# The inverse of Q's magnitude as a power of minus one on GpSimd instead of reciprocals on VectorE

## The chip, the cores and the metric

The kernel runs on one core of a Trainium2 chip. A core has TensorE (matrix products into PSUM banks; its weight loads are shown as PEld), VectorE (DVE), ScalarE (ACT), GpSimd (POOL), and a queue engine SyncE (SP) that starts transfers. The engines run their own instruction streams in order and wait for each other through semaphores. The metric is the device time of one execution in microseconds (us).

## The reference

Input x is 2 x 4096 tokens of 512 numbers, fp32. Two residual layers:

- Attention by binding: `y = layernorm(x)`; `Q, K, V = unit(y W + b)`, where `unit(f)` goes to the frequency domain, divides by `|f| + 1e-8` and comes back; `out = unbind(cumsum(bind(K, V)), Q)`, where bind and unbind are products of spectra (with the conjugate for unbind), and the running sum goes over the 4096 tokens of a sequence; `x = x + out`.
- Feed-forward: `layernorm(x)` times W_in gives 8 trees of 255 nodes each; the signs of the logits pick one path of 8 nodes in each tree; the silu of the logits on the path times W_out is added to x.

The kernel folds the Fourier transform into the projection weights, so the projections give real and imaginary parts directly, and everything up to the running sum and its product with Q stays in the frequency domain.

## The kernel before

8192 tokens are done in 32 blocks of T = 256. A step `step(s, ...)` works on three blocks at once: it projects block n = s + 1 and forms its running sum (`proj`), transforms block s back and adds the residual (`inv`), and does the feed-forward of block i = s - 1 (`ffn`). The first three steps (s = -1, 0, 1) and the last four are written out, those between run in a loop. All 32 steps with `proj` do what follows; 30 of them also have `ffn`. The order of the work on each engine is that of the code; nothing reorders it.

TensorE, in a step: the projections of Q, K and V (L416, banks `bank_p`), the inverse transform of block s (`bank_i`), then the trees: for t = 0 to 7, logits of tree t (L455, 24 products), and one tree later the counts of tree t (L464, products of the path matrix with the decisions `dec`), then the output products (L480). So counts of tree 0 come right behind the logits of tree 1.

The magnitudes, for q in Q, K, V (256 tokens times 2 groups of frequencies, 128x512 in `mag`): ScalarE takes the real and imaginary parts out of PSUM (L569 to L580) and squares them (L589, `square`); GpSimd adds the two squares (L783, `sum_squares`); ScalarE takes the square root (L593, `root`). For Q and K GpSimd adds epsilon (L788, `add_eps`). K's and V's magnitudes are multiplied and inverted on VectorE (L875, L881, `kv_denominator`, `kv_inverse`). Q's is inverted by two reciprocals of 128x256 on VectorE (L869, `q_inverse`), and GpSimd multiplies Q by it (L806, L807). The squares share one buffer, so `square` of the next of Q, K, V waits for `sum_squares` of the one before.

ScalarE's order in a step: parts and square of Q, real part of K, root of Q, rest of K and its square, real part of V, root of K, rest of V and its square, root of V, then the copy `odd` (L730) of half the inverse transform, then the silus of the eight trees.

VectorE's order in a step: low halves of the layer norm (L863), the two reciprocals for Q, `unfold` (L968 to L977, it needs `odd`), the decision of tree 0 (L948, `decide`), the residual (L982 to L986), the decision of tree 1, K's and V's denominator, and so on with decisions, low halves of the activations (L954), running sums (L911, L914).

GpSimd's order in a step: `sum_squares` and `add_eps` of Q, the same for K, the two multiplications of Q (they wait for the reciprocals), `sum_squares` of V, then the products of K and V (L816 to L819), and those of Q with the running sum (L824 to L835). In the first step a reduction over the partitions (L774) for the scale of the last weights stands between `add_eps` of Q and `sum_squares` of K.

Of the kernel before, what the change touches and what calls it, by code (L numbers as in the profile page):

```python
# [5 lines left out]
P = 128  # L6
# [4 lines left out]
T = 256  # L11
# [19 lines left out]
ALU = mybir.AluOpType  # L31
ACT = mybir.ActivationFunctionType
F32 = mybir.dt.float32
F16 = mybir.dt.float16
# [17 lines left out]
Q, K, V, G_IN, G_OUT = range(5)  # L52
# [14 lines left out]
def build(nc, x, wq, wk, wv, b_qkv, w_in_t, b_in_t, w_out_t, dft, table_hi, table_lo, table_sp, path_d,  # L67
          flags, keep_d, out):
    with ExitStack() as ctx:  # L69
        def sb(name, shape, dt=F32):  # L70
            return ctx.enter_context(nc.sbuf_tensor(name, shape, dt))
# [29 lines left out]
        s_act = sb("s_act", [P, 1])  # L101
        s_out = sb("s_out", [P, 1])
        off = sb("off", [P, 1])

        mx = sb("mx", [P, GROUPS, 2, 6])
        mxp = sb("mxp", [P, GROUPS])
# [8 lines left out]
        def take(words):  # L115
            spot[0] += words
            return arena[:, spot[0] - words:spot[0]]
# [3 lines left out]
        mag = take(3 * 2 * T).rearrange("p (x c t) -> p x c t", x=3, c=2)  # L121
# [83 lines left out]
        consts_done = sem("consts_done")  # L205
# [24 lines left out]
        den_ready = sem("den_ready")  # L230
        kv_den_ready = sem("kv_den_ready")
        rinv_ready = sem("rinv_ready")
# [530 lines left out]
        @block.gpsimd  # L763
        def _(pool):
            pool.memset(mx[:, :, :, :], 0.0).then_inc(cleared, 1)
            pool.memset(ln_eps[:, :], LN_EPS * X_SCALE ** -2).then_inc(cleared, 1)
            pool.memset(sp_raw[:, :], 1.0)
            pool.memset(zero[:, :], 0.0)
            pool.memset(carry[:, :], 0.0)
            pool.memset(sp_carry[:, :], 0.0).then_inc(cleared, 1)  # L770

            def over_partitions(g):
                pool.wait_ge(grp_max, g + 1)
                pool.partition_all_reduce(mxa[:, g:g + 1], mxp[:, g:g + 1], P, RMAX).then_inc(grp_all, 1)  # L774

            for g in (Q, K, V, G_IN):
                over_partitions(g)

            pool.wait_ge(wf_lo_done, 3)

            def sum_squares(n, q):
                pool.wait_ge(sq_ready, 3 * n + q + 1)
                pool.tensor_tensor(mag[:, q].rearrange("p c t -> p (c t)"), sq[:, 0:2].rearrange("p c t -> p (c t)"), sq[:, 2:4].rearrange("p c t -> p (c t)"), ALU.add).then_inc(ss_ready, 1)  # L783

            def add_eps(n, q):
                pool.wait_ge(consts_done, 1)
                pool.wait_ge(root_ready, 3 * n + q + 1)
                pool.tensor_scalar(mag[:, q], mag[:, q], eps_s[:, q:q + 1], 1.0 / ROOT_DOWN, ALU.add,  # L788
                                   ALU.mult).then_inc(den_ready, 1)

            def step(s, proj, inv, ffn, near, far):
                n = s + 1
                if proj:
                    sum_squares(n, Q)
                    add_eps(n, Q)
                    if not inv:
                        over_partitions(G_OUT)
                    if inv:

                        pool.wait_ge(kv_den_ready, n)
                    sum_squares(n, K)
                    add_eps(n, K)

                    pool.wait_ge(rinv_ready, 2 * n + 2)
                    pool.tensor_tensor(raw[:, Q, 0:2], raw[:, Q, 0:2], mag[:, Q], ALU.mult)  # L806
                    pool.tensor_tensor(raw[:, Q, 2:4], raw[:, Q, 2:4], mag[:, Q], ALU.mult).then_inc(q_hat_ready, 1)  # L807
                    sum_squares(n, V)

                    pool.wait_ge(k_hat_ready, n + 1)  # L810
                    kr, ki, vr, vi = raw[:, K, 0:2], raw[:, K, 2:4], raw[:, V, 0:2], raw[:, V, 2:4]
                    if inv:

                        pool.wait_ge(z_hi_ready, 2 * n)
                        pool.wait_ge(z_lo_ready, n)
                    pool.tensor_tensor(prod[:, 0], kr, vr, ALU.mult)  # L816
                    pool.tensor_tensor(prod[:, 1], ki, vi, ALU.mult)
                    pool.tensor_tensor(prod[:, 2], kr, vi, ALU.mult)
                    pool.tensor_tensor(prod[:, 3], ki, vr, ALU.mult).then_inc(bound, 1)  # L819

                    pool.wait_ge(cum_ready, n + 1)
                    pool.wait_ge(q_hat_ready, n + 1)
                    qr, qi, sr, si = raw[:, Q, 0:2], raw[:, Q, 2:4], cum[:, 0:2], cum[:, 2:4]
                    pool.tensor_tensor(prod[:, 0], sr, qr, ALU.mult)  # L824
                    pool.tensor_tensor(prod[:, 1], si, qi, ALU.mult)
                    pool.tensor_tensor(prod[:, 2], si, qr, ALU.mult)
                    pool.tensor_tensor(prod[:, 3], sr, qi, ALU.mult).then_inc(z_prod, 1)
                    pool.wait_ge(z_prod, n + 1)
                    pool.tensor_tensor(prod[:, 0], prod[:, 0], prod[:, 1], ALU.add)
                    pool.tensor_tensor(prod[:, 2], prod[:, 2], prod[:, 3], ALU.subtract).then_inc(z_sum, 1)  # L830
                    pool.wait_ge(z_hi_ready, 2 * n + 1)
                    pool.wait_ge(z_sum, n + 1)
                    pool.tensor_tensor(z_lo[:, 0:2], prod[:, 0], z_hi[:, 0:2], ALU.subtract)  # L833
                    pool.wait_ge(z_hi_ready, 2 * n + 2)
                    pool.tensor_tensor(z_lo[:, 2:4], prod[:, 2], z_hi[:, 2:4], ALU.subtract).then_inc(z_lo_ready, 1)  # L835

            steps(pool, step)

        @block.vector
        def _(dve):  # L840
# [18 lines left out]
            def low(b, xn, have, done):  # L859

                for j in range(J):
                    dve.wait_ge(have, J * b + j + 1)
                    dve.tensor_tensor(xn_pair[:, j, 1, :], xn[:, j, :], xn_pair[:, j, 0, :],  # L863
                                      ALU.subtract).then_inc(done, 1)

            def q_inverse(n, h):

                dve.wait_ge(den_ready, 2 * n + Q + 1)
                dve.reciprocal(mag[:, Q, h], mag[:, Q, h]).then_inc(rinv_ready, 1)  # L869

            def kv_denominator(n):

# [264 lines left out]
            def step(s, proj, inv, ffn, near, far):  # L1137
                n, i = s + 1, s - 1
                if near:
                    low(s + 2, xn1, xn1_hi_ready, xn1_lo_ready)  # L1140
                if proj:
                    for h in range(2):
                        q_inverse(n, h)
                if inv:
                    unfold(s)
                if ffn:
                    decide(i, 0)
                if inv:
                    residual(s)
                if ffn:  # L1150
                    decide(i, 1)
                if proj:
                    kv_denominator(n)
                    kv_inverse(n, 0)
                if ffn:
                    decide(i, 2)
                if proj:
                    kv_inverse(n, 1)
                if ffn:
                    act_low(i, 0)  # L1160
                    decide(i, 3)
                if proj:
                    k_scale(n)
                    if not inv:
                        for c in range(PIECES):
                            win_low(c)
                if ffn:
                    act_low(i, 1)
                    decide(i, 4)
                    act_low(i, 2)  # L1170
                if inv:
                    stats(s, x1, st2, mv2, ln2_stat, ln2_mv)
                if ffn:
                    decide(i, 5)
                    act_low(i, 3)
                    decide(i, 6)
                    act_low(i, 4)
                    decide(i, 7)
                    act_low(i, 5)
                if proj:  # L1180
                    running_sum(n)
                if ffn:
                    act_low(i, 6)
                    act_low(i, 7)
                if proj:
                    special_unit(n)
                    special_sum(n)
                    special_product(n)
                if proj and not inv:
                    wout_low(0)  # L1190
                    wout_low(1)
                if inv and not ffn:
                    wout_low(2)
                    wout_low(3)
                if inv:
                    scale_and_shift(s, mv2, rs2, nb2, ln2_std, ln2_rstd, ln2_nb)
                    low(s, xn2, xn2_hi_ready, xn2_lo_ready)
                if ffn:
                    result(i, 0)
                if far:  # L1200
                    dve.wait_ge(x_loaded, 16 * (s + 4))
                    stats(s + 3, xa, st1, mv1, ln1_stat, ln1_mv)
                    scale_and_shift(s + 3, mv1, rs1, nb1, ln1_std, ln1_rstd, ln1_nb)
                if ffn:
                    result(i, 1)
# [82 lines left out]
```

## Time and profile before

| | |
|---|---|
| median of 3 runs | 2157.69 us (2157.49 to 2158.01) |
| profiled execution | 2157.28 us |
| its span in the trace | 2155.3 us |
| TensorE busy | 2030.2 us (94%) |
| VectorE busy | 1446.2 us (67%) |
| ScalarE busy | 1179.5 us (55%) |
| GpSimd busy | 805.5 us (37%) |

The span is the time from the first to the last instruction in the trace; the execution's own time is 2.0 us longer. "Busy" is the time in which an engine works on an instruction, and idle time has a releaser: the instruction whose semaphore ended the wait. The granted clock of TensorE is 1.0 at 2.4 GHz and 0.5 at 1.2 GHz. The profile follows the chain that ended last back from the last instruction; through most of the span it runs over TensorE, whose products stand back to back. The first 220 us, in which weights are folded and split and the first blocks fill the pipeline, have long idle stretches on TensorE; behind them it is full.

### The profile page before, as it was taken

What the parts mean: (1) busy time and instruction counts of PE and PEld (TensorE: products, weight loads), DVE (VectorE), ACT (ScalarE), POOL (GpSimd) and SP (SyncE); (2) the same over time, 40 slices, a digit from 0 to 9 for tenths busy, and PEclk for the clock granted to TensorE, in tenths of its full rate; (3) what the DMA queues carried; (4) which work ended last, traced back from release to release, by engine and by line L of the source; (5) the groups of instructions that cost most, each with busy time, mean ns of one, the idle gap of its engine ahead of it and who ended that gap; (6) DMA issues with size and microseconds to landing.
All of it is one profiled execution on the core that took longest, in us unless ns stands there. A gap on an engine that the chain in (4) does not pass through costs nothing. (4 is left out here: it accounts for less than half of the span.)

```text
span 2155.3 us, 40151 instructions
## 1 busy us (share of the span) xinstructions
PE 2030.2 (94%) x15360; PEld 1477.8 (69%) x15360; DVE 1446.2 (67%) x2223; ACT 1179.5 (55%) x1994; POOL 805.5 (37%) x623
## 2 busy tenths in 40 slices
PE   7513999999999999999999999999999999999999
PEld 4312777777777777777777777777777777777766
DVE  3776666667777666677776666777766667777652
ACT  3443565555555655555556555555565555555642
POOL 0054434343344343433443434334434343344310
PEclk9856999999999999999999999999999999999999
DMA  7301122211211222112112221121122211211110
GB/s 270 102 16 33 37 60 59 58 49 49 58 24 53 58 58 58 49 49 58 24 53 58 58 58 49 49 58 25 53 58 58 58 49 49 58 25 45 40 45 25
DMA packets 174212, 118.30 MB, mean 55 GB/s; under 512 B 138466, under 2 KB 138850, under 8 KB 173666
## 3 DMA queue, kind: packets, MB, share of 16 engines
q1 hardware_dynamic: 174178, 117.83, 19.1%
q8 instruction: 23, 0.38, 0.1%
q14 instruction: 11, 0.09, 0.0%
HBM read 50.69 MB, written 16.78 MB: 31 GB/s over the span
## 5 line engine op out<-in xcount | busy, mean ns | idle before, releaser
L455 PE MATMUL bank_l<-arena,win_mem 128*128 128x256 f16 x6144 | 707.3, 273 | 0.0
L480 PE MATMUL bank_l<-wout_mem,arena 128*128 128x512 f16 x3072 | 673.5, 379 | 0.0
L455 PEld LDWEIGHTS bank_l<-arena,win_mem 128*128 128x128 f16 x6144 | 600.0, 98 | 69.0
L416 PE MATMUL bank_p<-arena,wf_hi 128*128 128x256 f16 x3072 | 514.7, 276 | 105.8 <-ACT arena L569 92.0
L480 PEld LDWEIGHTS bank_l<-wout_mem,arena 128*128 128x128 f16 x3072 | 300.6, 98 | 348.8
L416 PE MATMUL bank_p<-arena,wf_lo 128*128 128x256 f16 x1536 | 423.2, 276 | 0.0
L416 PEld LDWEIGHTS bank_p<-arena,wf_hi 128*128 128x128 f16 x3072 | 303.4, 99 | 151.8 <-ACT arena L569 80.2
L603 ACT ACTIVATE arena<-bank_l,bias_in,s_logit 128x256 f32<-128x256 f32 x512 | 260.9, 560 | 263.2 <-PE bank_l L464 263.2
L557 ACT ACTIVATE arena<-arena,nb,rs 128x512 f32<-128x512 f32 x128 | 97.1, 806 | 361.5 <-DVE nb L856 361.5
L954 DVE SCALAR_TENSOR_TENSOR arena<-arena,s_act 128x512 f16<-128x512 f32 x256 | 253.7, 1001 | 3.5 <-ACT arena L612 3.5
L783 POOL TENSOR_TENSOR arena<-arena 128x512 f32<-128x512 f32 x96 | 121.7, 1268 | 330.1 <-ACT arena L589 315.5
L869 DVE RECIPROCAL arena<-arena 128x256 f32<-128x256 f32 x64 | 107.7, 1724 | 191.3 <-POOL arena L788 191.3
L816 POOL TENSOR_TENSOR arena<-arena 128x512 f32<-128x512 f32 x32 | 56.0, 1750 | 407.5 <-DVE arena L887 407.5
L612 ACT ACTIVATE arena<-arena,s_act 128x512 f16<-128x512 f32 x256 | 184.8, 722 | 10.4
L948 DVE TENSOR_SCALAR dec<-bank_l,thr,off 128x256 bf16<-128x256 f32 x256 | 134.9, 527 | 47.4 <-PE bank_l L455 47.4
L416 PEld LDWEIGHTS bank_p<-arena,wf_lo 128*128 128x128 f16 x1536 | 152.0, 99 | 19.2
L968 DVE TENSOR_TENSOR arena<-bank_i,odd 128x254 f32<-128x254 f32 x32 | 13.5, 422 | 222.1 <-ACT odd L730 222.1
L863 DVE TENSOR_TENSOR xn_pair<-arena,xn_pair 128x512 f16<-128x512 f32 x128 | 82.7, 688 | 110.6 <-ACT xn_pair L564 110.6
L833 POOL TENSOR_TENSOR arena<-arena 128x512 f16<-128x512 f32 x32 | 39.1, 1223 | 207.6 <-ACT arena L750 207.6
L900 DVE TENSOR_TENSOR sp_hat<-sp_raw,sp_den 1x256 f32<-1x256 f32 x96 | 115.0, 1198 | 2.0
L824 POOL TENSOR_TENSOR arena<-arena 128x512 f32<-128x512 f32 x32 | 54.2, 1694 | 163.4 <-DVE arena L914 163.4
L881 DVE RECIPROCAL arena<-arena 128x256 f32<-128x256 f32 x64 | 111.6, 1746 | 1.1
(109 smaller groups left out, 2372.2 us busy)
## 6 DMA issues: line engine op xcount, KB each, us to landing
arena<-in_x SPq DMA_DIRECT2D x64, 512.0 KB, 3.4
arena<-arena SPq DMA_DIRECT2D x32, 512.0 KB, 3.2
out<-arena SPq DMA_DIRECT2D x64, 256.0 KB, 2.1
wout_mem<-in_w_in_t SPq DMA_DIRECT2D x1, 4096.0 KB, 22.0
win_mem<-in_w_out_t SPq DMA_DIRECT2D x1, 4096.0 KB, 21.1
arena<-in_w_out_t SPq DMA_DIRECT2D x1, 4096.0 KB, 17.2
arena<-xn_pair SPq DMA_TRANSPOSE x128, 3.2
arena<-in_dft SPq DMA_DIRECT2D x1, 1024.0 KB, 4.9
```

The lines of the kernel that those rows point to most:

```text
L416: mm = pe.matmul(bank, a, b, start=(n == 0), stop=(n == len(pairs) - 1))
L455: mm = pe.matmul(bank_l[t % 4][:, c * T:(c + 1) * T], a[:, k, w:w + P], x2t[:, :, b, k, :], start=(c == 0 and k == 0 and m == 0), stop=(c ...
L480: mm = pe.matmul(bank_l[j][:, :], a[:, m, tok], w[:, m, :], start=(m == 0 and a is a_hi and w is wout_hi), stop=(m == 2 * TREES - 1 and a ...
L557: act.activation(dst[:, j, :], src[:, j, :], ACT.Identity, bias=nb[:, j:j + 1], scale=rs[:, j:j + 1]).then_inc(done, 1)
L603: ins = act.activation(acts[:, t % HELD, c * T:(c + 1) * T], bank_l[t % 4][:, c * T:(c + 1) * T], ACT.Silu, bias=bias_in[:, c, t:t + 1], s ...
L612: act.activation(a_hi[:, 2 * t:2 * t + 2, :], acts[:, t % HELD, :].rearrange("p (c t) -> p c t", c=2), ACT.Copy, scale=s_act[:, 0:1]).then ...
L783: pool.tensor_tensor(mag[:, q].rearrange("p c t -> p (c t)"), sq[:, 0:2].rearrange("p c t -> p (c t)"), sq[:, 2:4].rearrange("p c t -> p ( ...
L869: dve.reciprocal(mag[:, Q, h], mag[:, Q, h]).then_inc(rinv_ready, 1)
L881: dve.reciprocal(mag[:, V, h], mag[:, V, h]).then_inc(kv_rinv_ready, 1)
L900: ins = dve.tensor_tensor(sp_hat[0:1, q, :], sp_raw[s, :], sp_den[s, :], ALU.mult)
L948: dve.tensor_scalar(dec[:, t % HELD, :], bank_l[t % 4][:, 0:T], thr[:, t:t + 1], off[:, 0:1], ALU.is_gt, ALU.mult).then_inc(dec_ready, 1)
L954: dve.scalar_tensor_tensor(out=a_lo[:, m, :], in0=acts[:, t % HELD, :].rearrange("p (c t) -> p c t", c=2), scalar=s_act[:, 0:1], in1=a_hi[ ...
```

## The change

The two reciprocals of Q's denominator leave VectorE. In their place GpSimd raises the whole 128x512 to the power of minus one, element by element, with an exponent tile `minus_one` (128x512 fp16, filled once at the start), directly behind `add_eps` of Q. GpSimd's multiplications of Q then wait for GpSimd's own power.

```diff
--- before.py
+++ after.py
@@ -101,6 +101,7 @@
         s_act = sb("s_act", [P, 1])
         s_out = sb("s_out", [P, 1])
         off = sb("off", [P, 1])
+        minus_one = sb("minus_one", [P, 2, T], F16)
 
         mx = sb("mx", [P, GROUPS, 2, 6])
         mxp = sb("mxp", [P, GROUPS])
@@ -765,6 +766,7 @@
             pool.memset(mx[:, :, :, :], 0.0).then_inc(cleared, 1)
             pool.memset(ln_eps[:, :], LN_EPS * X_SCALE ** -2).then_inc(cleared, 1)
             pool.memset(sp_raw[:, :], 1.0)
+            pool.memset(minus_one[:, :, :], -1.0)
             pool.memset(zero[:, :], 0.0)
             pool.memset(carry[:, :], 0.0)
             pool.memset(sp_carry[:, :], 0.0).then_inc(cleared, 1)
@@ -788,12 +790,17 @@
                 pool.tensor_scalar(mag[:, q], mag[:, q], eps_s[:, q:q + 1], 1.0 / ROOT_DOWN, ALU.add,
                                    ALU.mult).then_inc(den_ready, 1)
 
+            def q_inverse(n):
+                pool.wait_ge(consts_done, 1)
+                pool.wait_ge(den_ready, 2 * n + Q + 1)
+                pool.tensor_tensor(mag[:, Q], mag[:, Q], minus_one[:, :, :], ALU.pow).then_inc(rinv_ready, 1)
 
             def step(s, proj, inv, ffn, near, far):
                 n = s + 1
                 if proj:
                     sum_squares(n, Q)
                     add_eps(n, Q)
+                    q_inverse(n)
                     if not inv:
                         over_partitions(G_OUT)
                     if inv:
@@ -802,7 +809,7 @@
                     sum_squares(n, K)
                     add_eps(n, K)
 
-                    pool.wait_ge(rinv_ready, 2 * n + 2)
+                    pool.wait_ge(rinv_ready, n + 1)
                     pool.tensor_tensor(raw[:, Q, 0:2], raw[:, Q, 0:2], mag[:, Q], ALU.mult)
                     pool.tensor_tensor(raw[:, Q, 2:4], raw[:, Q, 2:4], mag[:, Q], ALU.mult).then_inc(q_hat_ready, 1)
                     sum_squares(n, V)
@@ -862,11 +869,6 @@
                     dve.wait_ge(have, J * b + j + 1)
                     dve.tensor_tensor(xn_pair[:, j, 1, :], xn[:, j, :], xn_pair[:, j, 0, :],
                                       ALU.subtract).then_inc(done, 1)
-
-            def q_inverse(n, h):
-
-                dve.wait_ge(den_ready, 2 * n + Q + 1)
-                dve.reciprocal(mag[:, Q, h], mag[:, Q, h]).then_inc(rinv_ready, 1)
 
             def kv_denominator(n):
 
@@ -1138,9 +1140,6 @@
                 n, i = s + 1, s - 1
                 if near:
                     low(s + 2, xn1, xn1_hi_ready, xn1_lo_ready)
-                if proj:
-                    for h in range(2):
-                        q_inverse(n, h)
                 if inv:
                     unfold(s)
                 if ffn:
```

On GpSimd, the loop's step from the sum of squares of Q (L783) to the two multiplications of Q (L806, L807), before. TENSOR_SCALAR is `add_eps`:

```order
77 L783 TENSOR_TENSOR arena<-arena 128x512
78 L788 TENSOR_SCALAR arena<-arena,eps_s 128x512
79 L782 REGISTER_ALU
80 L783 TENSOR_TENSOR arena<-arena 128x512
81 L788 TENSOR_SCALAR arena<-arena,eps_s 128x512
82 L805 ISA
83 L806 TENSOR_TENSOR arena<-arena 128x512
84 L807 TENSOR_TENSOR arena<-arena 128x512
```

The same place after the change:

```order
81 L785 TENSOR_TENSOR arena<-arena 128x512
82 L790 TENSOR_SCALAR arena<-arena,eps_s 128x512
83 L795 ISA
84 L796 TENSOR_TENSOR arena<-arena,minus_one 128x512
85 L784 REGISTER_ALU
86 L785 TENSOR_TENSOR arena<-arena 128x512
87 L790 TENSOR_SCALAR arena<-arena,eps_s 128x512
88 L812 REGISTER_ALU
89 L813 TENSOR_TENSOR arena<-arena 128x512
90 L814 TENSOR_TENSOR arena<-arena 128x512
```

The power (L796) has come between epsilon of Q and the sum of squares of K; the order is otherwise the same.

On VectorE, the same step before, from the low half of the layer norm (L863) to the decision of tree 0 (L948):

```order
229 L863 TENSOR_TENSOR xn_pair<-arena,xn_pair 128x512
230 L868 ISA
231 L869 RECIPROCAL arena<-arena 128x256 x2
232 L966 REGISTER_ALU
233 L968 TENSOR_TENSOR arena<-bank_i,odd 128x2x127
234 L969 TENSOR_TENSOR arena<-bank_i,odd 128x2x127
235 L970 TENSOR_TENSOR arena<-odd,bank_i 128x2x127
236 L971 TENSOR_TENSOR arena<-odd,bank_i 128x2x127
237 L974 REGISTER_ALU
238 L976 TENSOR_TENSOR arena<-bank_i,odd 128x2x2
239 L977 TENSOR_TENSOR arena<-bank_i,odd 128x2x2
240 L942 ISA
241 L948 TENSOR_SCALAR dec<-bank_l,thr,off 128x256
```

After the change the two reciprocals (row 231) are gone there, and the unfolding follows the low half.

## Rows read from the trace of the kernel before

**Rows 1.** The page: busy time, 40 slices and granted clock of TensorE.
```profile
PE 2030.2 (94%) x15360; PEld 1477.8 (69%) x15360; DVE 1446.2 (67%) x2223; ACT 1179.5 (55%) x1994; POOL 805.5 (37%) x623
...
PE   7513999999999999999999999999999999999999
...
PEclk9856999999999999999999999999999999999999
```

**Rows 2.** Timeline of GpSimd, middle step: start us, us, what [idle before <- releaser].
```profile
1025.59 0.69 POOL L788 TENSOR_SCALAR arena<-arena,eps_s 128x512 f32<-128x512 f32 x1 [0.83 <-ACT arena L593]
1028.88 1.27 POOL L783 TENSOR_TENSOR arena<-arena 128x512 f32<-128x512 f32 x1 [2.59 <-ACT arena L589]
1030.98 0.69 POOL L788 TENSOR_SCALAR arena<-arena,eps_s 128x512 f32<-128x512 f32 x1 [0.83 <-ACT arena L593]
1031.75 1.27 POOL L806 TENSOR_TENSOR arena<-arena 128x512 f32<-128x512 f32 x1
...
1034.21 1.27 POOL L783 TENSOR_TENSOR arena<-arena 128x512 f32<-128x512 f32 x1
```

**Rows 3.** Timeline of ScalarE, the same step.
```profile
1030.18 0.63 ACT L593 ACTIVATE arena<-arena 128x512 f32<-128x512 f32 x1 [0.47 <-POOL arena L783]
...
1035.51 0.63 ACT L593 ACTIVATE arena<-arena 128x512 f32<-128x512 f32 x1 [1.17 <-POOL arena L783]
1036.04 0.58 ACT L730 ACTIVATE odd<-bank_i 128x512 f32<-128x512 f32 x1
```

**Rows 4.** Timeline of VectorE, then TensorE's weight loads, the same step.
```profile
1026.32 3.36 DVE L869 RECIPROCAL arena<-arena 128x256 f32<-128x256 f32 x2 [5.96 <-POOL arena L788]
1036.72 0.42 DVE L968 TENSOR_TENSOR arena<-bank_i,odd 128x254 f32<-128x254 f32 x1 [7.04 <-ACT odd L730]
...
1038.19 0.53 DVE L948 TENSOR_SCALAR dec<-bank_l,thr,off 128x256 bf16<-128x256 f32 x1
...
1038.78 0.11 PEld L464 LDWEIGHTS bank_l<-dec,path 128*128 128x128 f16 x2 [0.37 <-DVE dec L948]
```

**Rows 5.** Waits, whole span: engine line <- releaser: us in total, times, longest.
```profile
POOL mxa L774 <- DVE mxp L1040: 79.4, 4, 44.8
...
PEld bank_l L464 <- DVE dec L948: 19.1, 60, 0.4
```

**Rows 6.** Timeline of GpSimd, steps of blocks 0, 1 and 2.
```profile
100.31 0.38 POOL L774 PARTITION_ALL_REDUCE mxa<-mxp  x1 [6.36 <-issue]
107.55 1.26 POOL L783 TENSOR_TENSOR arena<-arena 128x512 f32<-128x512 f32 x1 [6.86 <-issue]
...
168.17 1.27 POOL L783 TENSOR_TENSOR arena<-arena 128x512 f32<-128x512 f32 x1 [3.09 <-ACT arena L589]
...
228.49 1.27 POOL L783 TENSOR_TENSOR arena<-arena 128x512 f32<-128x512 f32 x1 [3.27 <-ACT arena L589]
```

**Rows 7.** Groups by line: out<-in shapes xcount | busy us, mean ns | idle before.
```profile
L783 POOL TENSOR_TENSOR arena<-arena 128x512 f32<-128x512 f32 x96 | 121.7, 1268 | 330.1 <-ACT arena L589 315.5
L869 DVE RECIPROCAL arena<-arena 128x256 f32<-128x256 f32 x64 | 107.7, 1724 | 191.3 <-POOL arena L788 191.3
...
L863 DVE TENSOR_TENSOR xn_pair<-arena,xn_pair 128x512 f16<-128x512 f32 x128 | 82.7, 688 | 110.6 <-ACT xn_pair L564 110.6
```

**Rows 8.** TensorE after three idle stretches; then windows: us, PE busy, PEclk, DMA.
```profile
46.20 14.14 PE L410 MATMUL bank_l<-arena 128*128 128x512 f32 x29 [6.30 <-ACT arena L618]
...
67.48 0.38 PE L416 MATMUL bank_p<-arena,wf_hi 128*128 128x256 f16 x2 [2.42 <-issue]
...
85.28 0.59 PE L416 MATMUL bank_p<-arena,wf_hi 128*128 128x256 f16 x2 [12.41 <-ACT arena L569]
...
46.20:50.20 4.00, 4.00 (x6) 0.64 0.00 0
67.48:71.48 4.00, 4.00 (x37) 1.00 0.00 0
85.28:91.28 6.00, 6.00 (x34) 0.60 0.95 249
```

## The prediction

> **What bounds the kernel now.** I read the page first. TensorE is busy 94% of the span, and from the fifth of the forty slices on it shows nines in time and in granted clock [rows 1]: time is lost only where something makes TensorE wait. The kernel repeats one step (a block of 256 tokens is projected while an older one is in the feed-forward part); 32 steps project a block, and in 30 of them the decision trees run too. So I looked for the chain inside a step that ends nearest to TensorE, with the timelines of one middle step.
>
> The chain runs over Q, K and V in turn. GpSimd adds the squares (L783), ScalarE takes the root (L593), GpSimd adds epsilon (L788). For Q that ends at 1025.59 + 0.69 = 1026.28. GpSimd then has nothing until ScalarE has squared K: it idles 2.59 us and starts L783 of K at 1028.88. From there it has no gap worth the name: root of K at 1030.18, epsilon at 1030.98, two multiplications from 1031.75, sum of squares of V at 1034.21 to 1035.48 [rows 2]. The root of V waits for exactly that (1.17 us of idle on ScalarE, released by L783), and behind it in ScalarE's order stands the copy `odd` at 1036.04 [rows 3]. VectorE's unfolding (L968) waits for `odd` at 1036.72, the first tree decision (L948) stands behind the unfolding at 1038.19, and TensorE's first count (L464) waits for the decision, 0.37 us of idle at 1038.78 [rows 4]. Over the steady part TensorE's weight loads wait for a decision 60 times, two in each of 30 steps, never over 0.4 us [rows 5]. The chain thus has no slack at its end: it already holds TensorE up a little. A microsecond of delay on GpSimd behind 1028.88 is a microsecond of TensorE's idle, and nothing gives it back, since everything later in the step follows from TensorE's logits or from the same VectorE order, and TensorE is the engine that is full.
>
> **The change, part by part.** *Removed from VectorE:* two reciprocals of 256 columns a step, 64 in all, 107.7 us busy [rows 7]. In the middle step they take 3.36 us from 1026.32, with 5.96 us of idle ahead; the next work on VectorE is L968, which comes 7.04 us after their end, released by ScalarE [rows 4]. Their removal widens an idle stretch. Worth: 0.
>
> *Removed wait:* the two multiplications by Q's inverse needed the reciprocals; these were done at 1029.68, and GpSimd reached the first multiplication at 1031.75 [rows 2, 4]. Worth: 0.
>
> *Added, small:* a memset of 128x512 fp16 at the start, where GpSimd next waits for maxima from VectorE, 79.4 us in four waits [rows 5]; covered. Two waits on semaphores that are long done or that its own previous instruction sets; between two GpSimd instructions tied so, a gap of about 0.08 us stands (1031.67 to 1031.75, [rows 2]). I take 0.08 with the power.
>
> *Added, large:* one power of 128x512 on GpSimd a step, 32 in all, between epsilon of Q and L783 of K. Call its duration p. In a middle step the idle of 2.59 us covers it, less the 0.08: **2.5 us are free**, and what p has above them goes onto the chain just described. In the step of block 1 the idle there is 3.09, in that of block 2 it is 3.27 [rows 6], so 3.0 and 3.2 are free; in these two TensorE idles for other reasons, but the chain that starts it again is this one (denominators, products, running sum, second layer norm), so I count them in full. In the step of block 0 the partition reduction of the last weight group, and behind it L783, follow the epsilon without any wait for data (the gap to 107.55 is shown as "issue") [rows 6], and VectorE waits for that reduction: nothing is free, all of p counts. For p above 3.2:
>
> added = p + (p − 3.0) + (p − 3.2) + 29 × (p − 2.5) = 32 p − 79 us (rounded).
>
> **What is p?** The trace has no power. The nearest rows bound it, from far apart. Low end: GpSimd adds or multiplies 128x512 in 1.268 us [rows 7], and if a power were done at that rate, p = 1.27. In between: VectorE takes 1724 ns for the reciprocal of 256 columns, 3.45 us for 512, against 688 ns for its subtraction of 512 (L863) [rows 7]: an inverse is 5.0 times a plain operation there. At 5.0 × 1.27, p = 6.4. But a power with its exponent read element by element isn't an inverse: arithmetically it is a logarithm, a product and an exponential. If the logarithm and the exponential cost 5 plain operations each and the product one, p = 11 × 1.27 = **14.0 us**. High end: single precision needs a series of some eight terms for each; with a plain operation a term, 17 × 1.27 = 21.6. The add and multiply on GpSimd show no hardware for anything better than a plain operation at 2.5 ns a column, so I expect the function to be made of such operations, and take the 14.0.
>
> **TensorE's clock.** TensorE would idle 14.0 − 2.5 = 11.5 us in mid-step. The trace shows what idle stretches of that kind do at the start [rows 8]: after 2.42 us the granted clock was 1.00 at once (2.4 GHz), after 6.30 us it was 0.64 over the next 4.0 us, after 12.41 us 0.60 over the next 6.0 us, both with time at the 1.2 GHz level. Lost: 4.0 × 0.36 = 1.4 us and 6.0 × 0.40 = 2.4 us. I take the mean, 1.9, for 30 steps: 57 us. In the first two steps TensorE restarts at half clock as it is.
>
> **Sum.** Exactly: 14.0 + 11.0 + 10.8 + 29 × 11.5 = 369.3; with 57, 426 us. The profiled execution took 2157.28 us (a span of 2155.3 and 2 us around it); 2157.3 + 426 = 2583.6, and since the median of the runs is 0.4 above it, **2584 us** (+20%).
>
> **The rivals.**
> *Power at the plain rate: not slower.* p of 1.3 to 2.5. All of it sits in the idle of 2.59 us; only block 0's step pays. At 1.27: 2157.7 + 1.3 = 2159. It decides at p = 2.56, where 29 × 0.06 + 2.6 passes 0.2% of the time, 4.3 us, which is about what a measurement of this kernel can tell from no change. For it: GpSimd shows one duration for addition and multiplication alike. Against: an inverse costs five times as much even on VectorE. A gain has no place to come from, since both things removed lie in idle time. 6%, same or, rarely, faster.
> *Power at the price of an inverse:* p of 2.6 to 9, at 6.4: 32 × 6.4 − 79 = 126. TensorE's idle is then 3.9 us, between the 2.42 that left the clock and the 6.30 that didn't, so 2284 to 2341. Same place, same wait. 24%.
> *A long software function:* p above 19, at 21.6: 612 + 57 = 669, 2827 us. For it: double steps for full precision, loads of coefficients, passes over a scratch. 23%.
> *The delay doesn't arrive:* TensorE might be reached by less than the chain's delay because it does other work first, or the change doesn't do what it says. The timeline shows TensorE at the count with its loads already waiting, so I give 2%, for any time from 2158 to the forecast.
>
> **How the numbers follow.** Forecast (p of 9 to 19, that is 2423 to 2743 by the formula with the 57): 45%. The range of 8 in 10 must reach into both neighbours: 2280 (p of 6.3, clock kept) to 2900 (p of 24) takes in about 18 of the 24, 45, and 16 of the 23. Slower by over 0.2%: 91%; within 0.2%: 7%; faster: 2%.
>
> **What the changed profile would show.** Right: a GpSimd row for the new line, 32 times, at 9 to 19 us; the idle of GpSimd ahead of L783 of K gone; the wait of L464 for the decision at p − 2.5 in each of 30 steps; steps longer by that and by 1 to 2.5 us; a granted clock that falls in each step; VectorE's wait for `odd` longer, while the other waits of the step keep their lengths. The forecast is wrong in size if the new row lies elsewhere, and in kind if the row is long and TensorE's wait at the count is much less than p − 2.5, or if another engine's wait takes the lead.

## The result, and the profile after

The changed kernel takes 4770.4 us (median of 4 runs, 4769.83 to 4772.23) against 2157.85 us before: the ratio is 2.211, with a 95% interval of 2.207 to 2.215. It is slower by 2613 us. The forecast was a time of 2584 us, 426 us above before, with a range from 2280 to 2900 us. The direction and the path were as forecast, the price of the power was not: 82.04 us where 14.0 was taken.

The page after, TensorE, the slices and the costliest groups (out<-in shapes xcount | busy, mean ns | idle before, releaser):

```profile
PE 2103.9 (44%) x15360; PEld 1521.5 (32%) x15360; DVE 1317.0 (28%) x2159; ACT 1179.5 (25%) x1994; POOL 3430.5 (72%) x656
...
PE   5011555333555333555333555333555334555339
...
POOL 2788776788766788766788766788766788666781
PEclk8555777666777666777667777667777667777669
...
L796 POOL TENSOR_TENSOR arena<-arena,minus_one 128x512 f32<-128x512 f32 x32 | 2625.5, 82046 | 3.0
L465 PE MATMUL bank_l<-dec,path 128*128 128x256 bf16 x512 | 104.5, 288 | 2385.2 <-DVE dec L950 2385.2
L970 DVE TENSOR_TENSOR arena<-bank_i,odd 128x254 f32<-128x254 f32 x32 | 13.5, 422 | 2979.9 <-ACT odd L731 2979.9
...
L594 ACT ACTIVATE arena<-arena 128x512 f32<-128x512 f32 x96 | 60.4, 629 | 2639.7 <-POOL arena L785 2639.7
```

TensorE's nines of before [rows 1] have become threes and fives, its clock a six or seven. The big idle figures of TensorE, VectorE and ScalarE are in the main one wait, seen from three engines. The timeline of GpSimd in a middle step answers to [rows 2]:

```profile
960.80 82.04 POOL L796 TENSOR_TENSOR arena<-arena,minus_one 128x512 f32<-128x512 f32 x1
1042.82 1.26 POOL L785 TENSOR_TENSOR arena<-arena 128x512 f32<-128x512 f32 x1
1044.91 0.69 POOL L790 TENSOR_SCALAR arena<-arena,eps_s 128x512 f32<-128x512 f32 x1 [0.83 <-ACT arena L594]
...
1048.13 1.27 POOL L785 TENSOR_TENSOR arena<-arena 128x512 f32<-128x512 f32 x1
```

ScalarE, VectorE and TensorE's weight loads in the same step, as in [rows 3, 4]:

```profile
1044.11 0.63 ACT L594 ACTIVATE arena<-arena 128x512 f32<-128x512 f32 x1 [79.97 <-POOL arena L785]
...
1049.43 0.63 ACT L594 ACTIVATE arena<-arena 128x512 f32<-128x512 f32 x1 [1.81 <-POOL arena L785]
1049.96 0.58 ACT L731 ACTIVATE odd<-bank_i 128x512 f32<-128x512 f32 x1
...
1050.58 0.42 DVE L970 TENSOR_TENSOR arena<-bank_i,odd 128x254 f32<-128x254 f32 x1 [95.80 <-ACT odd L731]
...
1052.04 0.54 DVE L950 TENSOR_SCALAR dec<-bank_l,thr,off 128x256 bf16<-128x256 f32 x1
...
1052.63 0.13 PEld L465 LDWEIGHTS bank_l<-dec,path 128*128 128x128 f16 x2 [79.79 <-DVE dec L950]
```

The idle of 2.59 us ahead of K's sum is gone, and from that sum to the count it is the chain of before, link for link: 9.81 us from 1042.82 to 1052.63, against 9.90 from 1028.88 to 1038.78 [rows 2, 4]. TensorE's wait at the count has grown from 0.37 to 79.79 us, by 79.42. The sum says 82.04 + 0.08 − 2.59 = 79.53.

The whole difference can be booked. The first count of tree 0 comes at 479.58 instead of 238.38 us: 241 us more, and the formula has 82.1 + 79.1 + 78.9 = 240 for the three steps ahead of it. From there to the last of the 30 counts that wait, 29 steps take 143.35 us each instead of 61.57, 2371.6 us more. Each holds 79.42 us of wait; the other 2.36 us are put down to the slow clock behind the wait. The stretch from that last count to the end is 2.4 us longer, and the sum is 2615, the difference of the spans. The pages of the profile agree on the clock's part: the same 15360 products kept TensorE busy for 2103.9 us instead of 2030.2, 73.7 more.

### The profile page after: what moved, and what is told of

Same layout as the page of the kernel before. It is cut to its first block and busy times, and to the rows that moved or that the text cites. A ratio compares the mean times of both kernels' runs of the same rounds, so it can differ in the third digit from the quotient of the medians.

```text
span 4770.4 us, 40098 instructions
## 1 busy us (share of the span) xinstructions
PE 2103.9 (44%) x15360; PEld 1521.5 (32%) x15360; DVE 1317.0 (28%) x2159; ACT 1179.5 (25%) x1994; POOL 3430.5 (72%) x656
## 5 line engine op out<-in xcount | busy, mean ns | idle before, releaser
L796 POOL TENSOR_TENSOR arena<-arena,minus_one 128x512 f32<-128x512 f32 x32 | 2625.5, 82046 | 3.0
L465 PE MATMUL bank_l<-dec,path 128*128 128x256 bf16 x512 | 104.5, 288 | 2385.2 <-DVE dec L950 2385.2
L970 DVE TENSOR_TENSOR arena<-bank_i,odd 128x254 f32<-128x254 f32 x32 | 13.5, 422 | 2979.9 <-ACT odd L731 2979.9
L465 PEld LDWEIGHTS bank_l<-dec,path 128*128 128x128 f16 x512 | 48.2, 99 | 2405.8 <-DVE dec L950 2393.5
L456 PE MATMUL bank_l<-arena,win_mem 128*128 128x256 f16 x6144 | 777.6, 289 | 0.0
L594 ACT ACTIVATE arena<-arena 128x512 f32<-128x512 f32 x96 | 60.4, 629 | 2639.7 <-POOL arena L785 2639.7
L481 PE MATMUL bank_l<-wout_mem,arena 128*128 128x512 f16 x3072 | 673.5, 379 | 0.0
L456 PEld LDWEIGHTS bank_l<-arena,win_mem 128*128 128x128 f16 x6144 | 637.5, 104 | 105.9
L481 PEld LDWEIGHTS bank_l<-wout_mem,arena 128*128 128x128 f16 x3072 | 300.8, 98 | 348.6
L956 DVE SCALAR_TENSOR_TENSOR arena<-arena,s_act 128x512 f16<-128x512 f32 x256 | 217.2, 858 | 3.5 <-ACT arena L613 3.5
```

The lines of the kernel that those rows point to most:

```text
L456: mm = pe.matmul(bank_l[t % 4][:, c * T:(c + 1) * T], a[:, k, w:w + P], x2t[:, :, b, k, :], start=(c == 0 and k == 0 and m == 0), stop=(c ...
L465: mm = pe.matmul(bank_l[t % 4][:, c * T:(c + 1) * T], path[:, c * P:(c + 1) * P], dec[:, t % HELD, :], start=False, stop=(c == 1), skip_gr ...
L481: mm = pe.matmul(bank_l[j][:, :], a[:, m, tok], w[:, m, :], start=(m == 0 and a is a_hi and w is wout_hi), stop=(m == 2 * TREES - 1 and a ...
L594: act.activation(mag[:, q], mag[:, q], ACT.Sqrt).then_inc(root_ready, 1)
L796: pool.tensor_tensor(mag[:, Q], mag[:, Q], minus_one[:, :, :], ALU.pow).then_inc(rinv_ready, 1)
L956: dve.scalar_tensor_tensor(out=a_lo[:, m, :], in0=acts[:, t % HELD, :].rearrange("p (c t) -> p c t", c=2), scalar=s_act[:, 0:1], in1=a_hi[ ...
```

## The experiments

The kernel before took 2158.4 us in the first set of runs (forms, four and eight products, power moved), 2157.5 in the second (two products, no power, copy moved) and 2157.0 in the third.

**What a power costs.** Powers and products of several forms on GpSimd, behind the last step of the kernel before, where nothing waits for them:

```diff
             steps(pool, step)
+            pool.wait_ge(z_lo_ready, NB)
+            pool.memset(bx, 3.0)
+            pool.memset(ex32, -1.0)
+            pool.memset(ex16, -1.0).then_inc(tried, 1)
...
+            for p, c, e in ((P, 512, ex16), (P, 512, ex32), (P, 256, ex16), (P, 128, ex16), (P, 64, ex16),
+                            (P, 16, ex16), (P, 8, ex16), (P, 1, ex16), (64, 512, ex16), (16, 512, ex16),
+                            (1, 512, ex16)):
+                form(ALU.pow, p, c, e)
+            for v, w in ((1.0, -1.0), (3.0, 2.0), (3.0, -0.5), (3.0, 0.0)):
...
+                form(ALU.pow, P, 128, ex16)
+            form(ALU.mult, P, 512, ex16)
```

> The kernel before, with powers and products of several shapes on GpSimd behind its last step, where nothing waits for them; only the durations of these instructions are read. The base is 3.0 and the exponent -1 unless told. Theory A (the power is a software function paid per column, 160 ns each): 128x512 at 82 us, 256 columns 41, 128 columns 20.5, 64 columns 10.3, 16 columns 2.6, 1 column well under 1 us; the same with 64, 16 or 1 partitions, since a core works on its own partitions side by side; the same with an fp32 exponent tile and for exponents 2, -0.5 and 0. Rival B (a price by instruction or a conversion of the fp16 exponent): durations that hardly fall with the columns, or far less than 82 us with the fp32 exponent. Rival C (it depends on the values): other durations for exponents 2, -0.5, 0 or base 1. A plain product of 128x512 stays at about 1.3 us.

Groups by shape on GpSimd behind 2063 us. A shape with several instructions mixes powers and products:

```profile
L853 POOL TENSOR_TENSOR arena<-arena 128x512 f32<-128x512 f32 x4 | 166.7, 41663 | 0.3
L853 POOL TENSOR_TENSOR arena<-arena 128x128 f32<-128x128 f32 x6 | 104.2, 17365 | 0.5
L853 POOL TENSOR_TENSOR arena<-arena 64x512 f32<-64x512 f32 x1 | 82.0, 82048 | 0.1
L853 POOL TENSOR_TENSOR arena<-arena 1x512 f32<-1x512 f32 x1 | 82.0, 82018 | 0.1
L853 POOL TENSOR_TENSOR arena<-arena 16x512 f32<-16x512 f32 x1 | 82.0, 82017 | 0.1
L853 POOL TENSOR_TENSOR arena<-arena 128x256 f32<-128x256 f32 x1 | 41.2, 41171 | 0.1
L853 POOL TENSOR_TENSOR arena<-arena 128x64 f32<-128x64 f32 x1 | 10.5, 10527 | 0.1
L853 POOL TENSOR_TENSOR arena<-arena 128x16 f32<-128x16 f32 x1 | 2.9, 2897 | 0.1
L853 POOL TENSOR_TENSOR arena<-arena 128x8 f32<-128x8 f32 x1 | 1.6, 1634 | 0.1
...
L853 POOL TENSOR_TENSOR arena<-arena 128x1 f32<-128x1 f32 x2 | 0.7, 368 | 0.2
```

And its timeline: the full width with the fp16 exponent, and powers of 128 columns with base 1.0 and exponent −1, then base 3.0 and exponents 2 and −0.5:

```profile
2064.44 82.10 POOL L853 TENSOR_TENSOR arena<-arena 128x512 f32<-128x512 f32 x1
...
2553.55 20.77 POOL L853 TENSOR_TENSOR arena<-arena 128x128 f32<-128x128 f32 x1
...
2574.81 20.74 POOL L853 TENSOR_TENSOR arena<-arena 128x128 f32<-128x128 f32 x1
...
2596.03 20.74 POOL L853 TENSOR_TENSOR arena<-arena 128x128 f32<-128x128 f32 x1
```

From 8 to 512 columns, the cost is about 0.35 us and 159.5 ns a column ((82.04 − 1.63) / 504). One partition costs as much as 128. Base 1.0 against 3.0 and the exponents −1, 2 and −0.5 make no difference. Exponent 0 doesn't either: the 128x128 shape holds five powers and one product in 104.2 us, and four powers at 20.75 leave 21.2 for the fifth and the product. Nor does the fp32 exponent: the 128x512 shape holds two powers and two products in 166.7 us, so both powers are at 82. Rivals B and C fall. The power is a fixed piece of work a column, about 65 times a plain operation (82.04 / 1.268). What it consists of no run shows.

**Nothing in its place.** The changed kernel without the power:

```diff
-                pool.tensor_scalar(mag[:, q], mag[:, q], eps_s[:, q:q + 1], 1.0 / ROOT_DOWN, ALU.add,
+                pool.tensor_scalar(mag[:, q], mag[:, q], eps_s[:, q:q + 1], ROOT_DOWN if q == Q else 1.0 / ROOT_DOWN, ALU.add,
...
-                    q_inverse(n)
...
-                    pool.wait_ge(rinv_ready, n + 1)
+                    pool.wait_ge(den_ready, 2 * n + Q + 1)
```

> The changed kernel without the power: VectorE has no reciprocals for Q, GpSimd has no power, and the inverse of Q's denominator is left out (Q is multiplied by the scaled denominator instead). It shows what the removal alone is worth. Theory A (both removed things lay in idle time): the time of the kernel before, 2157.7 within 0.2%. Rival B (VectorE's 3.36 us or the wait for the reciprocals were on the path): up to 107 us less.

Measured 2156.0 us, ratio 0.9990 (0.9981 to 0.9999): 1.5 us less, within 0.2%. The removal alone is worth next to nothing, as forecast; rival B falls.

**A known load in its place.** The kernel before, with k plain products on a tile of their own behind epsilon of Q (here k = 8):

```diff
+        one = sb("one", [P, 2, T], F16)
+        spent = sem("spent")
...
                     add_eps(n, Q)
+                    for r in range(8):
+                        if r:
+                            pool.wait_ge(spent, 8 * n + r)
+                        pool.tensor_tensor(one[:, :, :], one[:, :, :], one[:, :, :], ALU.mult).then_inc(spent, 1)
```

> The kernel before, with two plain products of 128x512 fp16 on a tile of their own in the power's place, in each of 32 steps. Theory A (2.5 us a step are free): p = 2.6, so 2.6 + 29 x 0.1 = 5 us, 2163 us, within 2160 to 2168. Rival C (nothing is free): 2157.7 + 83 = 2241 us.

> The kernel before, with four plain products of 128x512 fp16 on a tile of their own in the place where the power stood, in each of the 32 steps; VectorE keeps the reciprocals. Theory A (2.5 us free in a step, 3.0 and 3.2 in two, none in the first, the rest one to one onto TensorE): with 1.25 us each and their gaps p = 5.2, so 32 x 5.2 - 79 = 87 us, and with TensorE idle 2.7 us in a step no fall or a small one of the clock: 2245 to 2300 us. Rival B (the length of the chain is absorbed in part by other waits): less than 2210. Rival C (all of p counts in each step): 2324 or more.

> The same with eight products: p = 10.3. Theory A: 32 x 10.3 - 79 = 251, TensorE idles 7.8 us a step and loses about 2 us a step to the clock, 60: about 2470 us. Rival B: less than 2400. Rival C (all of p counts): 2540 or more.

An fp16 product takes 1.04 us and its successor starts 1.12 us behind it, so the loads are 2.16, 4.40 and 8.86 us, less than the expectations took. The loads of four and of eight in a middle step:

```profile
1004.38 4.40 POOL L803 TENSOR_TENSOR one<-one 128x512 f16<-128x512 f16 x4
```

```profile
1007.88 8.86 POOL L803 TENSOR_TENSOR one<-one 128x512 f16<-128x512 f16 x8
```

Measured, beside the formula 32 p − 79 with the load as p (for two products p alone, since only the first step pays):

| products | load, us | by the formula, without clock | time, us | above before | ratio |
|---|---|---|---|---|---|
| 2 | 2.2 | 2 | 2159.0 | 1.5 | 1.0006 (0.9997 to 1.0015) |
| 4 | 4.4 | 62 | 2248.5 | 90 | 1.0422 (1.0404 to 1.0439) |
| 8 | 8.9 | 205 | 2421.8 | 263 | 1.1222 (1.1207 to 1.1238) |

With two products TensorE waits for decisions exactly as it did before [rows 5]:

```profile
PEld bank_l L466 <- DVE dec L955: 19.1, 60, 0.4
```

With four and with eight the wait at the first count follows the load. In the trace with four products, then in that with eight:

```profile
310.51 0.11 PEld L466 LDWEIGHTS bank_l<-dec,path 128*128 128x128 f16 x2 [2.21 <-DVE dec L955]
...
373.93 0.11 PEld L466 LDWEIGHTS bank_l<-dec,path 128*128 128x128 f16 x2 [2.22 <-DVE dec L955]
...
438.86 0.11 PEld L466 LDWEIGHTS bank_l<-dec,path 128*128 128x128 f16 x2 [2.22 <-DVE dec L955]
```

```profile
1026.57 0.13 PEld L466 LDWEIGHTS bank_l<-dec,path 128*128 128x128 f16 x2 [6.65 <-DVE dec L955]
```

It rises by 1.84 with four (4.40 + 0.08 − 2.59 = 1.89) and by 6.28 with eight (8.86 + 0.08 − 2.59 = 6.35). Up to the 2.5 us a step the load is free; above, it goes one to one. Rival C falls. Rival B named limits (2210 and 2400) that both times exceed, and the one-to-one wait speaks against it. The forecast of 2470 for eight products was too high because its load was (10.3 against 8.86). What is above the third column, 28 and 58 us, is put down to the clock, read further down.

**A part of the power in the same place.** The power on 128 columns, reciprocals on VectorE for the other 384:

```diff
                     add_eps(n, Q)
+                    pool.wait_ge(den_ready, 2 * n + Q + 1)
+                    pool.tensor_tensor(mag[:, Q, 1, P:], mag[:, Q, 1, P:], minus_one[:, :], ALU.pow).then_inc(powered, 1)
...
-                dve.reciprocal(mag[:, Q, h], mag[:, Q, h]).then_inc(rinv_ready, 1)
+                w = P if h else T
+                dve.reciprocal(mag[:, Q, h, 0:w], mag[:, Q, h, 0:w]).then_inc(rinv_ready, 1)
```

> The kernel before, with the power in its place on the last 128 of the 512 columns, and VectorE's reciprocals on the other 384. Theory A (the power costs 0.35 us and 160 ns a column, and what is above 2.5 us a step goes one to one onto TensorE at the count of tree 0, with 2.3 us a step to the clock): p = 20.8; 20.8 + 17.8 + 17.6 + 29 x 18.3 = 587, and 66 for the clock: 2810 us; TensorE's wait at L464's count 18.5 us. Rival B (a long power in this place has a cost of its own, by the shared ports or by something it sets off, beside its length): more than 2850. Rival C (the formula holds only because the power was far above everything else; at 20 us other waits swallow part of it): less than 2770.

Measured 2805.9 us (ratio 1.301, 1.299 to 1.303), 4 us below theory A's 2810 and outside both rivals. Its power and its wait:

```profile
L801 POOL TENSOR_TENSOR arena<-arena,minus_one 128x128 f32<-128x128 f32 x32 | 664.3, 20758 | 2.7
```

```profile
PEld bank_l L466 <- DVE dec L955: 556.2, 30, 18.6
```

With a measured p and some 2.3 us a step for the clock, the formula of the prediction gives the time to 0.2%.

**The power behind the chain.** In the changed kernel, the power and Q's multiplications moved behind the sum of squares of V:

```diff
-                    q_inverse(n)
...
+                    sum_squares(n, V)
+                    q_inverse(n)
                     pool.wait_ge(rinv_ready, n + 1)
                     pool.tensor_tensor(raw[:, Q, 0:2], raw[:, Q, 0:2], mag[:, Q], ALU.mult)
                     pool.tensor_tensor(raw[:, Q, 2:4], raw[:, Q, 2:4], mag[:, Q], ALU.mult).then_inc(q_hat_ready, 1)
-                    sum_squares(n, V)
```

> The changed kernel with the power and Q's two multiplications moved behind the sum of squares of V. Theory A (the power costs through the chain Q, K, V, copy odd, decision, count): the count of tree 0 no longer waits; TensorE's wait moves to the inverse transform's input, at the end of GpSimd's step, and a step is GpSimd's own chain: 12 us from the sum of Q to that of V, 82, 2.5, 6.4, about 5 for the running sum, 9.3, 3 for the low halves, 7.4 to the next step: about 128 us in place of 143, the total about 4280 us. Rival B (the power adds its whole length wherever it stands): 4770 us or more. Rival C (GpSimd is bound only by its busy time of 107 us a step, the waits fill up): about 3600 us.

Measured 4312.5 us (ratio to before 1.998, 1.995 to 2.001), 458 us less than the changed kernel for one move. A step is 128.65 us (the powers start at 1023.15 and 1151.80). Both rivals fall. The place of the new wait, though, was misjudged. VectorE's wait for GpSimd at the running sum (L913), and the waits of TensorE's weight loads:

```profile
DVE arena L913 <- POOL arena L826: 2180.4, 32, 77.3
PEld bank_l L481 <- DVE arena L956: 1936.1, 30, 64.6
...
PEld bank_l L465 <- DVE dec L950: 14.1, 60, 0.3
```

The counts are free of it, and the wait stands at the output products (L481), not at the inverse transform: VectorE's order has the running sum ahead of the last two low halves of the activations, and the running sum waits for GpSimd (2180.4 us in 32 steps). One in-order engine passed the delay to work that doesn't need it, as ScalarE does in the changed kernel.

**The link out of the chain.** The kernel before, with the copy `odd` ahead of the root of V:

```diff
                     act.activation(sp_den[:, :], sp_raw[:, :], ACT.Abs).then_inc(sp_abs_ready, 1)
-                    root(n, V)
...
                     act.wait_ge(idft_full, J * (s + 1))
                     act.activation(odd[:, :, :], bank_i[:, :, COS_ODD.start:SIN_ODD.stop], ACT.Copy).then_inc(odd_ready, 1)
+                if proj:
+                    root(n, V)
```

> The kernel before, with ScalarE's copy odd ahead of the root of V, in place of behind it. Theory A (the chain through the root of V holds TensorE at the first counts, 0.3 to 0.4 us a step above the ordinary gap): the copy comes some 1.5 us earlier, the first decision too, and a part of the 19.1 us of waits at the counts goes: 2148 to 2154 us. Rival B (these waits are the ordinary hand-over between decision and count, no slack is missing): 2157.7 within 0.1%.

Measured 2143.2 us, ratio 0.9933 (0.9920 to 0.9947): 0.7% faster than before, and 5 us better than the expectation's near end, so that the gain was forecast in kind and too small. The first decision is made 1.5 us ahead of the count, and in its trace no count waits for a decision any more; the loads run on without idle:

```profile
1025.96 4.90 PEld L455 LDWEIGHTS bank_l<-arena,win_mem 128*128 128x128 f16 x45
1030.87 0.21 PEld L464 LDWEIGHTS bank_l<-dec,path 128*128 128x128 f16 x2
1031.09 2.61 PEld L455 LDWEIGHTS bank_l<-arena,win_mem 128*128 128x128 f16 x24
```

A step is 61.14 us instead of 61.57, and 29 × 0.43 = 12.5 of the 14.3 us are there. Rival B, that 0.37 us is an ordinary hand-over, falls: it was missing slack [rows 4, 5].

Then the same with the four products of 4.4 us:

> The kernel with the copy odd ahead of the root of V, and four plain products in the power's place (4.4 us a step), as in the run with four products. Theory A (what a delay on GpSimd costs is set by the one path sum of K, root of K, V, odd, decision; with odd moved this path has some 1.5 us of slack at TensorE and 0.7 us on ScalarE more): the delay of 1.9 us a step is swallowed, only the first steps pay: 2143 + about 7 = 2150 us, within 2145 to 2156. Rival B (the delay reaches TensorE by another path, the root and the denominators of V, or the clock still falls): 2200 us or more, the 91 us of the run with four products kept in good part.

Measured 2147.1 us, 4 us above the version without the products, where the same load had cost 90. ScalarE, middle step:

```profile
1029.71 0.63 ACT L595 ACTIVATE arena<-arena 128x512 f32<-128x512 f32 x1 [2.29 <-POOL arena L787]
...
1033.12 0.57 ACT L728 ACTIVATE odd<-bank_i 128x512 f32<-128x512 f32 x1
...
1035.06 0.63 ACT L595 ACTIVATE arena<-arena 128x512 f32<-128x512 f32 x1 [1.37 <-POOL arena L787]
```

The root of K still waits for GpSimd, 2.29 us; but `odd` no longer stands behind the root of V, and no wait for a decision is left on TensorE. So the cost of such a delay on GpSimd is set by the one path that the prediction named. (A power of 82 us would still hold up `odd`, through the root of K ahead of it in ScalarE's order; that wasn't run.)

## Why the prediction was wrong in size and right in place

- *What bounds the kernel, and the chain without slack:* right. The chain kept its length to 0.1 us, and the wait came where it was forecast, in 30 steps. This wasn't luck: four loads in the same place, from 2.16 to 20.8 us, and the two moves bear the path out.
- *Removals worth nothing:* right, 1.5 us without them.
- *2.5 us free in a step, nothing in the first, the rest one to one:* right. Two products cost 1.5 us in all (2.2 by the formula); four, eight, the partial and the whole power follow the formula. With p = 82.04 it gives 32 × 82.04 − 79 = 2546; with 2.36 × 30 = 71 for the clock 2617, measured 2613.
- *TensorE's clock, 1.9 us a step:* right in kind, a little low: 2.1 us after 6.65 us of idle (eight products), 2.2 after 18.6 (a part of the power), 2.36 after 79.8.
- *"What is p?":* this step failed. It took 14.0 us, called 21.6 a high end and let its range end at 24; measured 82.04, 5.9 times the first and 3.8 times the second. The 5.0 from VectorE's reciprocal was a row, but of another engine and another function. The eleven and seventeen plain operations were counted from arithmetic with no row under them. One plain operation for a term of a series was an assumption, and so was that nothing surrounds the series; the runs show some 65 plain operations' worth of time and not what fills it. The nearest rows bounded p from below; nothing in the trace bounded it from above, and the range should have stayed open there. The time came out 4770.4 − 2584 = 2186 us above the forecast, and 32 × (82.04 − 14.0) = 2177 are this one term.
- *The rule of the Trainium skill:* its three operations a cycle ("GPSIMD Engine Reference", section 3.1) gave 6.4 us with 45 operations, an estimate of the prediction. The rule bounds nothing without the number of operations, and here that was the unknown.
- *Rivals:* the plain rate, the price of an inverse and the long software function all had the right place and too small a price. The third was the nearest: its condition, p above 19, holds for 82.04, but it was priced at 21.6 and given 23%. The fourth, that the delay doesn't arrive, falls.

## What to carry to other kernels

Before an elementwise function goes to GpSimd, time it by itself. One instruction of 16 columns (2.90 us here) beside the 0.37 us of one column (the mean of a power and a product) would have told (2.90 − 0.37) × 32 = 81 us for 512. Where a trace has no row for an operation, the rows near it give a lower bound; leave the upper end open, above all for a function whose make-up no row shows. Moving work to an engine that is 37% busy is safe only up to the idle time ahead of the next instruction that others wait for (2.5 us of a step here), and an in-order engine behind it can hand the delay on to work that doesn't need it; a repair can be as small as moving one independent copy out of such a queue (14 us here).

## What the runs showed of the hardware that was not expected

- A power on GpSimd costs 0.35 us and 160 ns a column (8 to 512 columns), whatever the partitions (1 to 128), the type of the exponent, and the values tried.
- The granted clock after a short idle stretch is not decided by its length alone. With four products, TensorE idles 2.2 us in each step; windows of 4 us behind three such stretches (us, PE busy, clock, DMA):

```profile
310.60:314.60 4.00, 4.00 (x36) 1.00 0.01 3
374.00:378.00 4.00, 4.00 (x22) 0.57 0.09 9
438.90:442.90 4.00, 4.00 (x22) 0.57 0.05 13
```

  The first stayed at the 2.4 GHz level, the others fell to 1.2 GHz for a while and did 22 products instead of 36. The step behind the first takes 63.42 us, just the 1.84 us of wait above before, the next 64.93; of the 29 steps, 8 are of the first kind and 21 of the second. [rows 8] had an idle of 2.42 us without a fall. What decides it no run shows. The four executions took 2245.2, 2246.3, 2250.6 and 2255.1 us, and the longer ones had the lower mean granted clock (0.959, 0.959, 0.957, 0.955). TensorE's busy time for the same products, 33.5 us above before with four, 60.9 with eight and 73.7 with the power, tells what the clock cost in the profiled executions. After 79.79 us of idle it is 0.50, then 0.85:

```profile
1052.63:1056.63 4.00, 4.00 (x19) 0.50 0.01 3
1056.63:1060.63 4.00, 4.00 (x34) 0.85 0.35 129
```

- VectorE isn't held up beside the power. In the version with the power behind V's sum the power lies from 1023.15 to 1105.19, and VectorE's operations with two inputs run in it:

```profile
1024.38 0.42 DVE L970 TENSOR_TENSOR arena<-bank_i,odd 128x254 f32<-128x254 f32 x1 [15.73 <-ACT odd L731]
...
1033.76 0.65 DVE L956 SCALAR_TENSOR_TENSOR arena<-arena,s_act 128x512 f16<-128x512 f32 x1
```

  L970 took 0.42 us before too [rows 4]. The Trainium skill ("SBUF — State Buffer", section "Who interferes with whom") says that VectorE and GpSimd share a pair of SBUF ports behind an exclusive lock, and that a GpSimd instruction that reads SBUF and a VectorE instruction with two SBUF inputs contend for it, the one that comes second waiting for the whole of the first; `odd` is one such input here, the other comes from PSUM, but L956 reads both from SBUF, and took 0.65 us inside an 82 us power. For the power the measurement decides: a lock held through it would have kept L956 until 1105.19. Beside a plain operation of GpSimd both were slower, in the kernel before, where the same VectorE instruction is L954 and took 1.75 us, and GpSimd's took 1.69 instead of 1.27:

```profile
998.48 1.69 POOL L824 TENSOR_TENSOR arena<-arena 128x512 f32<-128x512 f32 x1 [5.26 <-DVE arena L914]
```

```profile
998.96 1.75 DVE L954 SCALAR_TENSOR_TENSOR arena<-arena,s_act 128x512 f16<-128x512 f32 x1
```
